# Narrow attention heads: compact values, six probability buffers, and value products in sections of 4, 3, 2 and 3 units

## The reference, cut to what matters

```
q, k, v = split(x @ c_attn_w)            # 16 heads of 8 channels
att = einsum('bhqd,bhkd->bhqk', q, k) / sqrt(8)
att = softmax(where(causal, att, -inf))
y = einsum('bhqk,bhkd->bhqd', att, v)
```

## Time and profile before

| | |
|---|---|
| median of 3 runs | 2647.75 us (2642.23 to 2649.84) |
| the profiled execution's own time | 2645.61 us |
| its span, first to last instruction | 2643.7 us |
| PE, DVE, ACT, POOL busy | 81%, 60%, 55%, 30% of the span |
| mean granted clock of TensorE | 0.895 |
| the first causal attention | from 1072 us |
| the windowed attention | from 1436 us |
| attention of the first block | 1600 to 1927 us |
| attention of the second block | 2166 to 2490 us |

### The profile page before, as it was taken

How to read it: one execution, slowest core, us unless ns; L and a number is a source line. 1 busy time by engine, 2 the same in 40 slices (tenths; PEclk the granted TensorE clock), 3 DMA queues, 4 the chain that set the end, 5 groups by cost and what they waited for, 6 DMA issues and landing times. The chain is left out here.

```text
span 2643.7 us, 37155 instructions
## 1 busy us (share of the span) xinstructions
PE 2140.0 (81%) x13716; PEld 1247.5 (47%) x13716; DVE 1591.2 (60%) x3477; ACT 1447.9 (55%) x2122; POOL 784.5 (30%) x428
## 2 busy tenths in 40 slices
PE   4999999999999538488346785999879737999798
PEld 3666666666666316122315342344347423444357
DVE  5978787787785465211564555777433666777324
ACT  3777777777777432598423243556653343555541
POOL 3877777687786002322003003000000031000000
PEclk7999999999999759699568796899989866999899
DMA  2000000000000310520501202211010012110010
GB/s 71 1 5 1 3 5 1 3 4 1 3 1 1 121 43 1 141 59 17 163 0 41 70 23 61 61 38 38 2 32 1 1 36 68 38 38 20 1 32 17
DMA packets 46411, 83.49 MB, mean 32 GB/s; under 512 B 11272, under 2 KB 19544, under 8 KB 43224
## 3 DMA queue, kind: packets, MB, share of 16 engines
q1 hardware_dynamic: 46232, 81.12, 11.2%
HBM read 64.09 MB, written 16.25 MB: 30 GB/s over the span
## 5 line engine op out<-in xcount | busy, mean ns | idle before, releaser
L713 ACT ACTIVATE probs<-psum_banks 128x1024 f32<-128x1024 f32 (+3 forms) x608 | 472.0, 827 | 357.3 <-PE psum_banks L581 258.6
L786 DVE TENSOR_REDUCE neg_max<-psum_banks 128x1 f32<-128x512 f32 (+3 forms) x672 | 398.5, 656 | 204.1 <-PE psum_banks L613 152.0
L1138 POOL TENSOR_SCALAR l0a_rows<-l0a_rows,l0a_rinv 128x1024 f32<-128x1024 f32 x160 | 454.4, 2845 | 188.8 <-DVE l0a_rinv L1100 185.1
L1088 DVE TENSOR_REDUCE l0a_nmax<-psum_banks 128x1 f32<-128x1024 f32 x256 | 312.4, 1220 | 137.7 <-PE psum_banks L982 135.7
L577 PE MATMUL psum_banks<-q_stack,k_stack 75*128 75x512 bf16 (+7 forms) x1216 | 295.6, 343 | 90.9 <-ACT probs L713 41.1
L1034 ACT ACTIVATE l0a_rows<-psum_banks,l0a_nmax 128x1024 f32<-128x1024 f32 x256 | 285.8, 1116 | 61.5 <-DVE l0a_nmax L1088 60.0
L609 PE MATMUL psum_banks<-k_stack,q_stack 72*128 72x128 bf16 (+3 forms) x1024 | 249.7, 327 | 79.3 <-DMA q_stack<-q_parts 67.2
L996 PE MATMUL psum_banks<-packed,l0a_rows 128*128 128x128 f32 x2048 | 266.2, 273 | 2.7 <-POOL l0a_rows L1138 1.6
L996 PEld LDWEIGHTS psum_banks<-packed,l0a_rows 128*128 128x128 f32 x2048 | 238.4, 141 | 42.9 <-issue 5.4
L981 PE MATMUL psum_banks<-l0a_kh,l0a_qw 128*128 128x512 f32 x512 | 241.1, 471 | 19.7 <-POOL l0a_qw L1127 13.5
L597 PE MATMUL psum_banks<-probs,v_ones 128*32 128x512 f32 (+3 forms) x2432 | 243.5, 515 | 7.7 <-ACT o_sum L682 6.5
(11 more groups left out here) (272 smaller groups left out, 3392.9 us busy)
## 6 DMA issues: line engine op xcount, KB each, us to landing
q_stack<-q_parts SPq DMA_DIRECT2D x72, 192.0 KB
k_stack<-k_parts SPq DMA_DIRECT2D x48, 192.0 KB
qkv<-in_l0f_w SPq DMA_DIRECT2D x6, 1024.0 KB, 5.5
q_parts<-parts SPq DMA_DIRECT2D x24, 256.0 KB, 3.3
k_parts<-parts SPq DMA_DIRECT2D x18, 256.0 KB, 4.9
moe_b<-in_l0f_b SPq DMA_DIRECT2D x32, 128.0 KB, 3.5
k_eight<-parts SPq DMA_DIRECT2D x16, 256.0 KB, 3.7
k_stack<-k_eight SPq DMA_DIRECT2D x16, 256.0 KB
```

The lines of the kernel that those rows point to most:

```text
L713: act.activation(S.Pt[:, U % PBUFS, 2 * half:2 * half + 2, c0:HALF], PS[:, bank:bank + 2, c0:HALF], ACT.Exp).then_inc(exp_done, 1)
L786: dve.tensor_reduce(out, scores, AX, ALU.max, negate=True).then_inc(job_read, 1)
L1088: dve.tensor_reduce(R.nmax4[:, s % 4:s % 4 + 1], scores(s), AX, ALU.max, negate=True).then_inc(max_done, 1)
L1138: rows_divided.mark(pool.tensor_scalar(R.Pr[:, s % RING, :], R.Pr[:, s % RING, :], R.rinv4[:, s % 4:s % 4 + 1], None, ALU.mult))
```

## The change

- `S.Vx` becomes a compact tile: per token tile 16 x 9 columns (eight values and a one per head) and 23 columns of zeros at the end, 167 in all. A head's weights are still 32 columns, from column 9 x head on; the columns beyond its nine are those of the following heads (or the zeros). POOL clears only the 23 columns and writes the ones without a wait between; the semaphore `zeroed` goes.
- With `use_max` the probability buffers are six instead of four. Without it they stay four.
- In the two causal stages with maximum (`use_max` and twelve units), the products with the values are made in sections: in the step in which U - LAG is 3, 6, 8 or 11 within the group, the last 4, 3, 2 or 3 units. Elsewhere they stay in pairs.

```diff
-PBUFS, LAG = 4, 2
+LAG = 2
+V_COLUMNS = NH * (HD8 + 1) + 32 - HD8 - 1
...
+    pbufs = 6 if use_max else 4
+    together = {3: 4, 6: 3, 8: 2, 11: 3} if use_max and nu == 12 else {u: 2 for u in range(1, nu, 2)}
...
-                    m = pe.matmul(PS[32 * i:32 * (i + 1), 7, c0:HALF], S.Vx[:, NT * b + kt, h0 + i, :],
-                                  S.Pt[:, U % PBUFS, i, c0:HALF], start=kt == 0, stop=u == last_unit(units, side),
+                    m = pe.matmul(PS[32 * i:32 * (i + 1), 7, c0:HALF], S.Vx[:, NT * b + kt, (HD8 + 1) * (h0 + i):(HD8 + 1) * (h0 + i) + 32],
+                                  S.Pt[:, U % pbufs, i, c0:HALF], start=kt == 0, stop=u == last_unit(units, side),
...
-                if 0 <= U - LAG < total and (U - LAG) % 2:
-                    values(U - LAG - 1)
-                    values(U - LAG)
+                if 0 <= U - LAG < total:
+                    for back in reversed(range(together.get((U - LAG) % nu, 0))):
+                        values(U - LAG - back)
...
-                        if U >= PBUFS and half == 0:
-                            act.wait_ge(pv_done, U - PBUFS + 1)
+                        if U >= pbufs and half == 0:
+                            act.wait_ge(pv_done, U - pbufs + 1)
...
-            pool.memset(S.Vx[:], 0.0).then_inc(zeroed, 1)
-            pool.wait_ge(zeroed, 1)
-            pool.memset(S.Vx[:, :, :, HD8:HD8 + 1], 1.0)
+            heads = S.Vx[:, :, 0:NH * (HD8 + 1)].rearrange("p t (h e) -> p t h e", e=HD8 + 1)
+            pool.memset(S.Vx[:, :, NH * (HD8 + 1):], 0.0)
+            pool.memset(heads[:, :, :, HD8:], 1.0)
             for b in range(B):
-                pool.tensor_copy(S.Vx[:, NT * b:NT * (b + 1), :, 0:HD8], V[:, b].rearrange("p t (h e) -> p t h e", e=HD8)).then_inc(v_ready, 1)
+                pool.tensor_copy(heads[:, NT * b:NT * (b + 1), :, 0:HD8], V[:, b].rearrange("p t (h e) -> p t h e", e=HD8)).then_inc(v_ready, 1)
...
-        S.Vx, S.parts = S.sb("v_ones", [P, TT, NH, 32]), S.sb("parts", [P, 2, 3, T], BF16)
-        S.Pt, S.Oc, S.rinv = S.sb("probs", [P, PBUFS, 4, HALF]), S.sb("o_sum", [P, 2, HALF]), S.sb("sum_inv", [P, 2, 4, 4])
+        S.Vx, S.parts = S.sb("v_ones", [P, TT, V_COLUMNS]), S.sb("parts", [P, 2, 3, T], BF16)
+        S.Pt, S.Oc, S.rinv = S.sb("probs", [P, 6 if use_max else 4, 4, HALF]), S.sb("o_sum", [P, 2, HALF]), S.sb("sum_inv", [P, 2, 4, 4])
```

More of the change, by code:

```diff
@@ L478, in four_heads @@
         (cols_ready, exp_done, masked, pv_done, evicted, job_ready, job_read, split_done, c_split, c_copied,
-         summed, part_done, rest_dve, rest_pool, zeroed, v_ready, ones_set) = sems[:17]
+         summed, part_done, rest_dve, rest_pool, v_ready, ones_set) = sems[:16]
         stored, loaded, c_loaded = sems[17:19], sems[19:23], sems[23:27]
@@ L712, in _ @@
                         bank = 2 * (n % pairs)
-                        act.activation(S.Pt[:, U % PBUFS, 2 * half:2 * half + 2, c0:HALF], PS[:, bank:bank + 2, c0:HALF], ACT.Exp).then_inc(exp_done, 1)
+                        act.activation(S.Pt[:, U % pbufs, 2 * half:2 * half + 2, c0:HALF], PS[:, bank:bank + 2, c0:HALF], ACT.Exp).then_inc(exp_done, 1)
                     if use_max and half == 0 and 0 <= U - LAG < total:
@@ L735, in _ @@
                     pool.wait_ge(exp_done, 2 * (U + 1))
-                    block_of = S.Pt[:, U % PBUFS, :, c0:c0 + P]
+                    block_of = S.Pt[:, U % pbufs, :, c0:c0 + P]
                     pool.affine_select(block_of, block_of, pattern=[[0, 4], [1, P]], compare_op=ALU.is_ge, fill=0.0, base=0,
```

## The result

The changed kernel takes 2742.96 us (median of 4 runs) against 2645.77 us of the kernel before beside it: ratio 1.036, interval 1.0334 to 1.0386, 97 us slower. The forecast was 2677 us, with a range up to 2710: the direction was right, the size was not. (One of the four runs was disturbed; the ratio leaves it out.) The profiled execution lasted 2737.36 us, 91.8 us more than that of before.

The account below looks back on a forecast made before the run. DVE with its gaps was taken as the bound, PE close behind. 14 groups x 2.1 us plus 2 x 0.5 made +30.4 us on 2645.6, 2676; adjusted to the runs' median 2678, stated as 2677, range 2650 to 2710.

Parts of the forecast that it names:

- DVE with its gaps is the bound at full clock: Steady groups of the two causal stages with maximum: DVE's gaps grow from 3.31 to 5.40 us, +2.1 us per group.
- The rival that PE is the bound: Steady groups: DVE's gaps get absorbed, 0.7 us less per group, -11 us in all, 2637 us; chance 0.15.
- The clock rival: Clock falls in PE's new 1.3 us wait: 2.3 us in each of 14 groups, 32 us more, 2709; chance 0.12.
- In which nothing in the change has a part: The chain from PE's turn to the next group, with four small DMAs, stays 4.82 us.
- Part 1 costs 0: Stage heads: compact values and the smaller GpSimd memset (6.92 us before) are off the path, cost 0.
- one of the prediction's own signs of being wrong: Forecast is wrong if the time moves in the stages whose order is unchanged.
- no contention: Stage heads: subtractions take 1222 ns beside the memset, 1226 without POOL work, so dropping the memset brings nothing back.
- off the path: Stage heads: POOL was done at 1610.07, PE began at 1620.03, held by DMA loads; cost 0.
- Part 2, buffers, costs 0: Six probability buffers: ACT gains nothing with pairs, and the new order needs them; cost 0.
- The last groups: Last group of each block, without row jobs, paced by ACT and PE in turn: +0.5 us, between -0.5 and +1.

Follow-up runs that it names:

- both idles filled: Changed kernel plus unused 512-column TensorE products, six before the turn's wait for the split and four at each group's start: 2685.9 us, ratio 1.0154.
- With DVE out of the way: Row maxima over 128 columns only: changed kernel with its sections 2641.05 us, the same with pairs in place of the sections 2604.92 us.
- kernel with the turn filled: Changed kernel plus six unused 512-column TensorE products before the turn's wait for the split: 2720.01 us, ratio 1.0283.
- pairs with six buffers and later copies: Changed kernel with value products in pairs again and GpSimd's value copies held until VectorE's four subtractions are done: 2644.85 us, ratio 0.9998.
- the kernel with the pair moved out of step 11: Changed kernel with pairs again, but units 8 and 9 moved from step 11 to step 1, joining 10 and 11: 2741.65 us, ratio 1.0372.
- the kernel with threes last: Changed kernel with sections of 2, 2, 2, 3 and 3 units instead of 4, 3, 2 and 3: 2666.68 us, ratio 1.0082.
- the one with the start filled: Changed kernel plus four unused 512-column TensorE products at each group's start, before the wait for the DMAs: 2706.84 us, ratio 1.0237.

## Why the prediction missed, point by point

1. *DVE with its gaps is the bound at full clock.* Right. Gaps of 2.02 and 2.39 for 2.00 and 2.37, groups of 36.0 us for 36.1 where the clock held (with both idles filled); other schedules also came out within about 0.1 us where the clock held, as long as the row maxima were whole.
2. *The rival that PE is the bound* (0.15): refuted, and by more than I thought. With DVE out of the way the sections are still 0.40 us per group slower, because they leave the split uncovered.
3. *The clock rival* (chance 0.12, 2.3 us per group, 2709): this is the step that failed. The forecast put the clock at nothing in its sum, and the rival that held it was wrong in three ways. Its price was that of one low section; measured are 6.7 us between a group at 0.87 (40.70) and one of before, of which 4.7 are clock (40.7 less 36.0), and 48.3 us over the 14 intervals for the rival's 32. A fall slows everything in the low stretch, some ten microseconds in most groups, not one section. Its chance rested on a single wait of 1.3 us at the turn; filling that wait gave back 23 of 57 us, filling the start 36. Some of the falls lie far from the turn, at the section of four. And the range ended at the rival's own centre.
4. *"In which nothing in the change has a part"*, said of the 4.82 us from turn to next group. True of the length, wrong of the content. Before, the section of 8 and 9 stood in it in step 11, between an idle of 0.45 us for ACT and that of 0.95:

```profile
1722.79 0.28 PE L577 MATMUL psum_banks<-q_stack,k_stack 75*128 75x256 bf16 x1 [0.45 <-ACT probs L713]
1723.61 1.71 PE L597 MATMUL psum_banks<-probs,v_ones 128*32 128x512 f32 x16
```

   After, the one of 7 and 8 stands in step 10. I summed columns there and not when they come, and the runs speak for the latter. After, the idles of 0.46 and 0.87 us both lie behind it, within 2.47 us (1776.02, the first product behind the section, to 1778.49). The kernel with the turn filled has these two idles and no wait at the turn, the same amount as before, and still falls to 0.87 in eight of twelve groups. That the order alone does it is read from this pair of kernels, which differ in the long sections too; it was not tried by itself.
5. *Part 1 costs 0*: wrong by 6 us in all, also in the first two of the four stages, whose order is unchanged (subtractions of 6.09 us for 4.71): one of the prediction's own signs of being wrong. I read the earlier trace rows as "no contention", but the memset there only writes. The sentence that everything on GpSimd is off the path was true of its end and not of what it runs beside. The Trainium skill (SBUF — State Buffer, Who interferes with whom) has it exactly: a VectorE instruction with two SBUF inputs contends with a GpSimd instruction that reads SBUF, not with one that only writes. The rows agree: 1222 ns beside the memset, up to 2058 beside the copies.
6. *Part 2, buffers, costs 0*: in line with ratio 0.9998 of pairs with six buffers and later copies.
7. *The last groups* (+0.5 each): +6.0 and -1.5 us measured; clock is in that too and I can't split it.

**What stays open.** What exactly TensorE must do to keep the clock, and what the emptied step 3 costs by itself. The runs order only roughly by the idle around turn and start that has no section within it: pairs (0.45 and 0.95 us on either side of one) and the kernels with both ends filled held the clock in their steady groups but for a single one here and there; the kernel with the pair moved out of step 11 (0.44, 0.31 and 2.22 in a row) lost most. But the kernel with threes last waits 1.56 us at the turn and loses some clock in five of twelve groups, while the one with the start filled waits 1.32 and loses some in every group. No single idle settles it, and the share of the short score products wasn't isolated.

## What to carry to other kernels

- When a change moves TensorE's work, ask what is left of its work inside each fixed round trip (here the turn and its four DMAs), not only whether the round trip gets longer. Ask the same of the steps that the moved work leaves behind. Where only short products and idle are left, price the loss as a whole low stretch (in this kernel half speed over some ten microseconds per group) and give it a chance far above 0.1.
- Removing a slow instruction on a side engine moves what is queued behind it. Look at which critical instructions it will then run beside.
- Filler work that does nothing but keep an engine busy is a cheap way to tell clock from geometry. Read the granted clock afterwards: fillers that end 9 us before the work they are meant for changed nothing here.

## What the runs showed of the hardware

- Adding ten products per group made the kernel 57 us faster (2743 to 2686), as the granted clock stayed at 1.00 in eleven of twelve steady groups.
- Idles of 0.46 and 0.88 us, with 1.1 us of short products around them, came before a fall in eight of twelve steady groups of the kernel with the turn filled. The Trainium skill (TensorE: Matmul & The Clock Gate, A second HAM failure mode: psum-queue depth-cycling) describes frequent short idles that make the clock swing; this trace agrees: 40.64 us at 0.87 beside 36.05 at 1.00 in one and the same kernel.
- A subtraction of 1222 ns took up to 2058 beside a GpSimd copy, and two copies 3.02 us instead of 2.02: both sides paid.
- In the changed kernel four waits of 0.15 to 0.21 us within 3 us came just before the fall at 1837.39. Nine of its twelve steady groups have a fall in this part of the group; the five kernels with pairs in steps 1 to 11 and whole row maxima have one in sixty.
